# Four graph layers on one core: one ring of twelve for masked scores and probabilities, the maxima pass writing back into its bank, and the planned order moved by constants

## What is computed

```python
# layer 0, one head                      layer 2 is the same with 4 heads of 64
h = x @ W
e = leaky_relu(s1[:, :, None] + s2[:, None, :], 0.2)
att = softmax(where(adj > 0, e, NEG))
x = layernorm(x + elu(att @ h))
# layer 1, 8 heads of 32: scores q k^T / sqrt(32), mask, softmax, values; two layer norms; an FFN between
# layer 3, one head
e = leaky_relu((x @ W1) @ (x @ W2)^T, 0.2)
att = softmax(where(adj > 0, e, NEG))
x = layernorm(x + relu(att @ (x @ W3)))
```

## Time and profile before

| | |
|---|---|
| runs | 2973.89 us median of 3 (2971.31 to 2974.82) |
| profiled execution | 2974.13 us, of which the span from first to last instruction is 2972.3 us |
| granted TensorE clock, mean | 0.981 |
| busy of the span | PE 93%, ACT 89%, DVE 86%, POOL 79%, PE weight loads 51% |
| HBM | 13 GB/s over the span |

### The profile page before, as it was taken

How to read it: one execution, slowest core, us unless ns; L and a number is a source line. 1 busy time by engine, 2 the same in 40 slices (tenths; PEclk the granted TensorE clock), 3 DMA queues, 4 the chain that set the end, 5 groups by cost and what they waited for, 6 DMA issues and landing times. The chain is left out here.

```text
span 2972.3 us, 69732 instructions
## 1 busy us (share of the span) xinstructions
PE 2773.1 (93%) x22576; PEld 1510.7 (51%) x22576; DVE 2560.7 (86%) x8261; ACT 2659.7 (89%) x5079; POOL 2345.3 (79%) x2517
## 2 busy tenths in 40 slices
PE   5999999999999999999999999999999999999855
PEld 4444445555555555545555554555555455554433
DVE  6778889889989888998989999898998889889764
ACT  6668889899999999999999999999989999898974
POOL 5467779788878888887888888788887888887774
PEclk9999999999999999999999999999999999999978
DMA  7355567767767767776676767677777777676565
GB/s 172 71 99 107 104 118 133 140 118 143 136 133 127 139 131 135 128 140 129 129 143 129 139 131 135 123 137 133 136 129 136 130 134 140 125 129 118 108 114 100
DMA packets 1215804, 378.91 MB, mean 127 GB/s; under 512 B 1157712, under 2 KB 1194320, under 8 KB 1215440
## 3 DMA queue, kind: packets, MB, share of 16 engines
q1 hardware_dynamic: 1213616, 373.46, 67.6%
q10 hardware_dynamic: 1824, 0.99, 0.2%
HBM read 21.43 MB, written 16.78 MB: 13 GB/s over the span
## 5 line engine op out<-in xcount | busy, mean ns | idle before, releaser
L910 POOL TENSOR_TENSOR split_r<-prob_r,split_r 128x512 f16<-128x512 f32 x768 | 880.5, 1159 | 275.8 <-DVE split_r L1385 272.9
L1349 DVE CUSTOM_DVE_ANT_0 unused<-bank_ps,neg_mask 128x512 bf16<-128x512 f32 x1024 | 661.7, 684 | 121.0 <-PE bank_ps L1561 120.3
L1627 PE MATMUL bank_ps<-val_r,trans_r 128*128 128x64 f16 (+1 forms) x9216 | 631.7, 222 | 72.9 <-DMA trans_r<-split_r 72.2
L1627 PEld LDWEIGHTS bank_ps<-val_r,trans_r 128*128 128x128 f16 x9216 | 526.9, 99 | 252.5 <-DMA trans_r<-split_r 74.8
L1154 ACT ACTIVATE prob_r<-bank_ps 128x512 f32<-128x512 f32 x1024 | 571.6, 607 | 48.7 <-PE bank_ps L1579 43.5
L1133 ACT ACTIVATE prob_r<-masked_r,low_r 128x512 f32<-128x512 f32 x768 | 535.8, 722 | 41.0 <-DVE low_r L1334 35.6
L1385 DVE TENSOR_SCALAR_CACHE_REDUCE split_r<-prob_r 128x512 f16<-128x512 f32 x768 | 510.9, 677 | 49.6 <-ACT prob_r L1133 25.7
L1587 PE MATMUL bank_ps<-prob_r,value_ones 128*33 128x512 f32 (+1 forms) x2048 | 546.1, 611 | 0.1
L1334 DVE CUSTOM_DVE_ANT_0 masked_r<-bank_ps,neg_mask 128x512 f32<-128x512 f32 x768 | 507.9, 683 | 31.0 <-ACT bank_ps L1122 22.9
L1578 PE MATMUL bank_ps<-stack 98*128 98x512 f16 x1024 | 393.3, 384 | 0.4 <-DVE low L1349 0.2
L1579 PE MATMUL bank_ps<-neg_mask_t,identb 128*128 128x512 bf16 x1024 | 389.6, 381 | 0.0
(11 more groups left out here) (148 smaller groups left out, 4532.7 us busy)
## 6 DMA issues: line engine op xcount, KB each, us to landing
stack<-qk SPq DMA_DIRECT2D x384, 128.0 KB, 2.4
xcur<-in_x_dram SPq DMA_DIRECT2D x32, 512.0 KB, 4.0
out_dram<-z SPq DMA_DIRECT2D x32, 512.0 KB, 3.1
trans_r<-split_r SPq DMA_TRANSPOSE x768, 3.3
xt_r<-split_r SPq DMA_TRANSPOSE x320, 3.3
stack<-low_rows SPq DMA_DIRECT2D x128, 4.0 KB
qk<-in_adj_dram SPq DMA_DIRECT2D x1, 1024.0 KB, 7.9
z<-in_L_gnn_W_dram SPq DMA_DIRECT2D x4, 256.0 KB, 12.3
```

The costliest lines, as they stand in the source:

```text
L910: nc.gpsimd.tensor_tensor(split_r[:, j, 1, :], prob_r[:, i, :], split_r[:, j, 0, :], ALU.subtract).then_inc(lo_done.sem, 1)
L1349: nc.vector.tensor_tensor_reduce(out=unused[:, nth % 2, :], in0=bank_ps[entry("bank", "sq", g, t, b, h)][:], in1=neg_mask[:, b, :], scale= ...
L1627: ins = nc.tensor.matmul(bank[:, at:at + width], trans_r[:, i, pp, jb, :], val(g, layer)[:, vp, jb, cols], start=(n == 0), stop=(n == len( ...
```

## The change

1. **One ring.** `masked_r` is gone. `prob_r` has 12 entries in place of 7. A unit opens its entry at `mk`, `ex` computes the exponential in place (input and output are the same entry), and `lo` closes it. The wait for the entry's former user moves from ACT (before `ex`) to DVE (before `mk`), and the wait of `mk` for an earlier `ex` goes.
2. **`mx` in place.** `mx` writes its full output in f32 into the PSUM bank that it reads. The tile `unused` and the wait for the `mx` two back go.
3. **Order by constants.** `schedule()` runs as before, with the old ring sizes, and gives only start times. A new `settle()` adds to each start a constant per kind (NUDGE) and one per place in the graph's list (OFFSET), the same for all graphs (DRIFT takes 0.1 us off for graph 0 alone), sorts all tasks by the moved start, and makes from that the five queues and the entries of all rings and banks: an opener gets the entry whose last user is planned to end first. PW_RUN = 0 leaves its branch out.

```diff
+    IN_RING = {"masked": "prob"}
+    RINGS = {**POOLS, "prob": 12}
...
+    NUDGE = {"add_0": -1, "add_1": -0.6, "add_3": 0.8, "ap_0": -0.5, "ap_1": -0.1, "ap_2": 1.1, "ap_ffn": 0.2, "ap_out": 0.4,
...
+             -0.2, "job_hi_f1": 0.3, "job_hi_g": 0.5, "job_hi_h2": -0.3, "job_hi_h3": 0.1, "job_hi_k": -2.7, "job_lo_f2": 0.1,
...
+             "job_lo_s2": -0.2, "job_q": 0.3, "job_s2": 1.2, "lo_0": -0.9, "lo_3": -0.7, "load": 4.9, "md": -2.4, "mh": -0.3,
+             "mk_0": 0.3, "mk_2": 0.1, "mr": 0.2, "mt": -0.3, "mx": 0.3, "nd": -1.8, "nm_0": -4, "nm_1": 0.4, "nm_3": 0.8,
+             "nm_ffn": -1.4, "nr": 1.2, "pv_0": -0.2, "pv_2": -0.1, "pv_3": -0.8, "pw": 0.3, "q_hi": -0.3, "q_lo": 1.7, "rc_0":
...
+             -0.5, "st_0": 0.5, "st_1": -0.5, "st_2": 1, "st_3": -0.2, "st_ffn": -0.6, "st_out": 1.5, "stack": 22, "store":
+             30.5, "tr_0": -0.2, "x_hi_0": 1, "x_hi_1": 2.1, "x_hi_2": -1.4, "x_hi_3": -0.8, "x_hi_ffn": 4.2, "x_lo_1": 0.7,
...
+    OFFSET = {0: -5.2, 1: -0.8, 4: 0.5, 5: -0.2, 6: 0.7, 13: -0.4, 15: 0.1, 16: -0.4, 18: 0.1, 19: 0.5, 20: 0.6, 21: 0.7, 22:
...
+              0.6, 75: -2.6, 76: -0.9, 77: 1.6, 78: -3.3, 79: -20.3, 80: 0.3, 81: 0.3, 84: -0.2, 85: -0.2, 87: 0.2, 89: 0.1, 91:
...
+              488: -1.3, 489: 0.3, 491: -14.7}
+    DRIFT = {0: -0.1}
+    PW_RUN = 0
...
-        return order, place, before, max(ends.values())
-
-    ORDER, PLACE, BEFORE, LENGTH = schedule()
+        return order, start, max(ends.values())
+
+    def settle(order, start):
...
+            moved[key] = begin + NUDGE.get(kind_of(key), 0) + OFFSET.get(nth - first[key[1]], 0) + DRIFT.get(key[1], 0) - ahead
+            for name, opener in closes:
+                closers.setdefault((IN_RING.get(name, name), opener), []).append(key)
+        place, before = {}, {}
+        entries = {name: [[-1e18, None, n] for n in range(size)] for name, size in RINGS.items()}
+        in_turn = sorted(tasks, key=lambda key: (moved[key], tasks[key][6][1]))
+        for key in in_turn:
+            for name, opener in tasks[key][3]:
+                name = IN_RING.get(name, name)
+                if (name, opener) in place:
+                    continue
+                entry = min(entries[name], key=lambda e: (e[0], e[2]))
+                place[name, opener], before[name, opener] = entry[2], entry[1]
+                entry[0] = max(moved[k] + tasks[k][1] + tasks[k][5] for k in closers[name, opener])
+                entry[1] = opener
+        return {engine: [key for key in in_turn if tasks[key][0] == engine] for engine in order}, place, before
...
-        unused = sb("unused", [P, 2, N], bf16)
...
-        masked_r = sb("masked_r", [P, POOLS["masked"], N])
-        low_r = sb("low_r", [P, POOLS["masked"]])
-        prob_r = sb("prob_r", [P, POOLS["prob"], N])
+        low_r = sb("low_r", [P, RINGS["prob"]])
+        prob_r = sb("prob_r", [P, RINGS["prob"], N])
...
-                    was = prior("prob", *unit)
-                    if was is not None:
-                        act.wait_ge(*prob_free(was))
                     act.wait_ge(*masked_done.at(*unit))
-                    i = entry("masked", *unit)
-                    nc.scalar.activation(prob_r[:, entry("prob", *unit), :], masked_r[:, i, :], ACT.Exp,
+                    i = entry("prob", *unit)
+                    nc.scalar.activation(prob_r[:, i, :], prob_r[:, i, :], ACT.Exp,
...
-                    i = entry("masked", *unit)
-                    was = prior("masked", *unit)
+                    i = entry("prob", *unit)
+                    was = prior("prob", *unit)
                     if was is not None:
-                        dve.wait_ge(*probs_done.at(*was))
+                        dve.wait_ge(*prob_free(was))
...
-                    nth = largest_done.at(g, t, b, h)[1]
-                    if nth > 2:
-                        dve.wait_ge(largest_done.sem, nth - 2)
+                    bank = bank_ps[entry("bank", "sq", g, t, b, h)][:]
                     eng.sem_inc(masking, 1)
-                    nc.vector.tensor_tensor_reduce(out=unused[:, nth % 2, :], in0=bank_ps[entry("bank", "sq", g, t, b, h)][:],
+                    nc.vector.tensor_tensor_reduce(out=bank, in0=bank,
```

More of the change, by code:

```diff
@@ L369, in schedule @@
         open_entries = {}
+        start = {}
         now, left = 0.0, len(tasks)
@@ L404, in schedule @@
                 order[engine].append(best)
+                start[best] = now
                 end = now + us
@@ L433, in schedule, with kind_of @@
                 now = events[0]
-        return order, place, before, max(ends.values())
-    ORDER, PLACE, BEFORE, LENGTH = schedule()
+        return order, start, max(ends.values())
+    def settle(order, start):
+        def kind_of(key):
+            return f"{key[0]}_{key[2]}" if key[0] in BY_STAGE else key[0]
+        moved, closers = {}, {}
+        for key, (_, us, _, _, closes, lands, (_, nth)) in tasks.items():
+            begin, ahead = start[key], 0.0
+            if key[0] == "pw" and PW_RUN > 1:
+                run = [(*key[:3], kb) for kb in range(key[3] // PW_RUN * PW_RUN, key[3] // PW_RUN * PW_RUN + PW_RUN)]
+                begin = max(start[k] for k in run)
+                ahead = 1e-4 * (tasks[run[-1]][6][1] - nth)
+            moved[key] = begin + NUDGE.get(kind_of(key), 0) + OFFSET.get(nth - first[key[1]], 0) + DRIFT.get(key[1], 0) - ahead
[14 more added lines that the diff above has]
+        return {engine: [key for key in in_turn if tasks[key][0] == engine] for engine in order}, place, before
+    PLANNED, START, LENGTH = schedule()
+    ORDER, PLACE, BEFORE = settle(PLANNED, START)
     print("planned", LENGTH, {e: round(sum(tasks[k][1] for k in ORDER[e])) for e in ORDER})
@@ L1327, in _ @@
                     layer, h, b = key
-                    i = entry("masked", *unit)
-                    was = prior("masked", *unit)
+                    i = entry("prob", *unit)
+                    was = prior("prob", *unit)
                     if was is not None:
-                        dve.wait_ge(*probs_done.at(*was))
+                        dve.wait_ge(*prob_free(was))
                     dve.wait_ge(*leaky_done.at(*unit))
                     eng.sem_inc(masking, 1)
-                    nc.vector.tensor_tensor_reduce(out=masked_r[:, i, :], in0=bank_ps[entry("bank", "sc", *unit)][:],
+                    nc.vector.tensor_tensor_reduce(out=prob_r[:, i, :], in0=bank_ps[entry("bank", "sc", *unit)][:],
                                                    in1=neg_mask[:, b, :],
```

## The result

The changed kernel takes 2965.39 us (median of 7 runs, 2961.80 to 2968.42), the kernel before 2971.77 us among the same runs: a ratio of 0.9976, 95% interval 0.9964 to 0.9987. Measured again beside others, it took 2964.63 us, ratio 0.9966 (0.9954 to 0.9978). So it is faster, by 0.24 to 0.34%, 6 to 11 us by the medians, where 34 us were forecast. The direction and the range held, the size did not.

A forecast was written before the change was run, and what follows sets the result against it. PE, busy 93% of the span, was taken as the bound, with 294 us lost by the sum of starts. DMA waits of 29 us plus 5 at the end made 34 us, from 2974.1 to 2940 us; range 2895 to 2992.

The forecast's parts named there:

- PE bounds the kernel, by many small stalls: Whole span: PE, busy 93%, is the bound; it loses 4.2 us per steady graph and no single wait carries it.
- sum of starts: PE's task costs, taken from start to start: 83.7 us per graph, 2678 us for 32, leaving 294 us open.
- Ring and `ex`, 0: Common ring and in-place exponential: 7.7 us of waits removed on ACT and DVE, 0 for PE; `ex` stays 722 ns.
- The unnamed 14.7 us: PE's waits of value `job` without a releaser, in the middle: nothing counted, as it may be the sequencer.
- `mx`, 0 to 6 ns, nothing on PE: Maxima pass on DVE writing its PSUM bank: at most 6 us of DVE in all, 0 on PE's path.
- Order in the middle, -29 us by two DMA waits: PE from 465 to 2790 us: later DMA consumers remove the visible waits of 17.3 + 11.5 us.
- Start and fill, 0: Pipeline filling before 465 us: the chain of graphs rules, reordering neighbours does little; no gain or loss counted.
- End, -5 us: After 2790 us: 5 of the 43.4 us that `pv` waits for the DMA are gained, an estimate.
- Moves the waits and no more: Rival on PE's waits: each removed one may be replaced by the next task's; within 6 us, near 2972; chance 0.10.
- The bank rival: PSUM banks held some 0.8 us longer between `sq` and `mx`, so `u` waits: slower, 3000 us; chance 0.19.

The follow-up runs named there:

- no_const: Changed kernel with all order constants multiplied by 0, keeping the ring of 12 and `ex` and `mx` in place: 2975.51 us, 1.0013 against the kernel before.
- mx_sbuf11: Changed kernel with `mx` back in its SBUF tile and a ring of 11 entries: 2961.11 us, 0.9967 against the kernel before.
- pe_only: Changed kernel with the constants applied to PE's tasks alone: 3097.69 us, 1.0429 against the kernel before.
- pwrun2: Changed kernel with PW_RUN = 2, which puts two `pw` of a pair together: 3022.69 us, 1.0177 against the kernel before.
- the three exchanges: mx_sbuf11 with `sq` moved behind a `pw` (70 places), ahead of two (70), or ahead of one (134): 2996.75, 2994.30, 3026.57 us.
- a passage of another shape: Changed kernel with the constants 0 up to graph 6, rising by a sixth per graph to 1 at graph 12: 2971.19 us.

## Why the prediction was right in sign and wrong in size

- **PE bounds the kernel, by many small stalls**: right, as far as the traces go. Over half of the steady gain lies inside its busy time. So far the trace agrees with the Trainium skill (page Perfetto Trace Analysis, section Identifying the Most-Contended Engine), by which busy time is a bad metric for matmuls: it is 2773 us here, above the sums of the starts. The page's reason is that such records look smaller in a trace, though, and here they look longer (0.38 us for a step of 0.22). The prediction's sum of starts was somewhat low, since it left out what a step between unlike tasks costs. I price every pair of neighbouring matmul kinds by the 10th percentile of its distances in the traces of both orders, a `pw` taken as one piece. By this estimate PE needs 2707 us in the old order and 2692 in the new one, so some 265 us were open and not 294. With other percentiles the difference between the orders is 12 to 16 us. Some 9 of the 15 us are steps at `pw`. It stands behind an `sq` 87 times and not 25, where it costs no more than a 16-bit task (315 ns, against 316 for `u`), while behind `u` it costs 0.09 us more; and the new order has 483 runs of `pw`, the old one 498.
- **Ring and `ex`, 0**: right. `ex` stays at 722 ns, neither it nor `mk` waits for an entry, and both together are 1.7 us of no_const, inside the noise.
- **The unnamed 14.7 us, "it may be the sequencer"**: wrong. They were waits for the transposing DMA (above), so the DMA waits of the middle were 44.0 us and not 29.
- **`mx`, 0 to 6 ns, nothing on PE**: wrong. It is 0.04 us from start to start where two `mx` stand together, 0.019 us on average, 20 us of DVE in all, and 3 to 6 us of the kernel. I took `em` as the nearest row because it writes f32 into its PSUM bank, but `em` has no accumulator output. The bound should have gone by what ends a pass: the row of the accumulator read, 84 ns before, is 143 ns after, and 83 again in mx_sbuf11. The "some 9 us of DVE idle per graph" didn't cover it, since DVE's largest wait is for `sq`, whose banks `mx` closes.
- **Order in the middle, -29 us by two DMA waits**: the step that failed in cause. These waits were to go and did not: counted by what ended them they were 44.0 us and are 41.5 and 38.6. The constants of `pv` and `job` alone (dma_users) leave them at the 38.7 us of no_const and lose 34 us against it. What the constants gave is, in 13 graphs, 11 us inside PE's busy time and 6 us of visible waits. The steady size came out near the forecast, 86.5 to 86.6 us per graph (1126.3 / 13, 1124.8 / 13) against 86.9, with another cause in the main, which is luck.
- **Start and fill, 0**: the step that failed in size. I had the steady rate gained from 465 us on and nothing lost before. Instead the passage into the new order costs some 8 to 10 us, and until the 16th graph nothing is gained: 29 us forecast for the middle, 16 found in it, less 10 at the start.
- **End, -5 us**: 9.0 us less waiting for the DMAs, of which 2 us reach the span.
- **Sum**: +10 to the 9th graph, 0 to the 16th, -16 to the 29th, -2 at the end gives -8, between the two measured -5.9 and -9.6. In it are 3 to 6 us that `mx` gives back.
- **The rivals.** "Moves the waits and no more" described the named waits well: all of PE's in the middle add up to 64.7 us before and 65.9 after. The measured gain lies just beyond its bound of 6 us. The bank rival did not decide this order. The waits of `sq` on `mx` doubled (15.2 to 32.9 us) and those of `u` fell, and what PE itself waited for `mx` rose from 7.7 to 14.4 us. But it is what the rows of pe_only, pwrun2 and the three exchanges show, and there the time lies 33 to 132 us above the version that each started from or the changed kernel: its price was real.

**Open**: what in the passage costs the 8 to 10 us, since a passage of another shape cost as much; why nothing is gained from the 9th to the 16th graph; how much of the gain inside PE's busy time is cheaper steps and how much short stalls (7 to 8 of the 17 us are steps by the estimate above, some 2 of work with them); and which moves carry the steady gain, since no part of them stands alone.

## What to carry to other kernels

In a kernel of strict queues that are nearly full, an order is worth something only as a whole: read the gain from marks of equal work in successive iterations, and price the passage into the new order by itself, since it can eat half of what the steady part gives. Don't take the named wait for the place where a new order gains; over half of the steady gain here was in time that the profile calls busy. Where a wait has no releaser in the profile, look at what ended just before it: here that turned 14.7 us of "issue" into waits for a DMA and 16.5 us into waits for ScalarE. Price a pass into another memory by a row of the same kind of operation, its accumulator read included.

## What was unexpected of the hardware

- A DVE pass over 128x512 with an accumulator output takes 713 ns with f32 output into PSUM and 684 with bf16 into SBUF, its accumulator read 143 and 84 ns, and the next pass starts 0.628 and 0.609 us later in the mean. The extra time stands only where two such passes into PSUM follow each other directly (0.648 us against 0.610). `mk`, the same operation with f32 into SBUF, took 685 ns and its accumulator read 85. `em`, the same shape into PSUM without an accumulator, took 690 ns.
- The f32 matmuls of `pw` start 0.31 us behind a 512-column matmul (1524.93 to 1525.24), where 16-bit ones follow each other at 0.22 us. This is 0.309 us in the median of all 286 such places, 0.123 us behind a 64-column matmul where 16-bit ones take 0.029, and two `pw` in a row take 1.86 us where two apart take 2.01. Behind `sq` the first matmul of a `pw` starts at 0.315 us, and so does a 16-bit one (0.316).
